# Cross-attention of a decoder layer: weighted sums in four groups of three chunks per batch, and a fourth buffer for the exponentials

## The chip, the cores and the metric

The kernel runs on one NeuronCore of one Trainium2 chip. The metric is the device time of one execution in microseconds (us); the median of three runs is compared. The engines are named as the profile names them: PE is TensorE's matmul stream and PEld its weight loads, DVE is VectorE, ACT is ScalarE, POOL is GpSimd, SP is SyncE, which here issues the DMAs.

## What is computed

One post-norm decoder layer on 32 batches of 56 tokens of 128 features: a self-attention, a cross-attention over 1500 context rows of 96 features, and a mixture of eight experts, each followed by a residual and a layer norm. The change lies in the cross-attention alone:

```python
q = (query @ Wq + bq).reshape(B, Nq, 16, 8).transpose(0, 2, 1, 3)
k = (key_value @ Wk + bk).reshape(B, Nkv, 16, 8).transpose(0, 2, 1, 3)
v = (key_value @ Wv + bv).reshape(B, Nkv, 16, 8).transpose(0, 2, 1, 3)
attn = jnp.clip(jnp.einsum('bhqd,bhkd->bhqk', q, k) * 8 ** -0.5, -CLAMP, CLAMP)
attn = jax.nn.softmax(attn, axis=-1)
x = jnp.einsum('bhqk,bhkd->bqhd', attn, v).reshape(B, Nq, 128)
return x @ Wo + bo
```

## The kernel before

The kernel has one instruction stream per engine, written out by hand, with a semaphore wait wherever one engine needs another. The cross-attention is a software pipeline of *periods*, one for each batch b (two more at the front and one behind). Each engine's function `period(b, par, half)` walks through twelve *slots*, c = 0 to 11, one for each *chunk* of 125 context rows. In slot c of period b, PE does the following in this order:

- **Scores** (L1063): four matmuls of 125 x 224 give the scores of chunk c into one of two pairs of PSUM banks. They wait until the exponential of chunk c-2 is done (semaphore `weights_ready`), since that frees the pair of banks.
- **Pieces** (L1049): the row maximum that softmax subtracts is found a batch ahead. It takes 21 *pieces* per batch, each one matmul of 128 x 500 into bank 0 or 1 and one reduction by DVE (L752, `taken`). The tables `EARLY_PIECES`, `MID_PIECES` and `LATE_PIECES` say which piece is done in which slot, and where in it: early is right after the scores, mid is after the projections, late is at the slot's end. There are only two banks, so piece n waits until the reduction of piece n-2 is done (`piece_max_taken`). Piece 1 uses bank 0 like piece 0 and waits for the reduction of piece 0. Piece 2 waits for `max_row_ready`.
- **Value projection** (L1088, slots 3, 9, 11) and **key projection** (L1097, slots 5, 6, 8) for a later batch. All of them write bank 7, as does the spread of the softmax sums (L1076, slot 0), which DVE inverts with two reciprocals (L775) in slots 0 and 1. The value projection of slot 3 waits until both reciprocals are done (`sums_inverted`).
- **The turn** (L1101, slot 8): a small matmul that transposes the row maxima, with 7 columns of weights. It waits for the last reduction of the row maxima (L763).
- **Weighted sums** (L1113 and L1117), chunk by chunk as the table `OUTPUTS` says: for chunk k four matmuls of 168 columns and four of 56, whose weights are 25 and 9 columns wide and which write the partitions from 0, 32, 64 and 96 of bank 6. They wait for the exponential of chunk k.

ACT in slot c takes the exponential of chunk c (L563) into the buffer `P2[c % NP]`, for which it waits until the weighted sum of chunk c - NP has been made; it also copies keys (L576, L578; slots 4, 6, 7) and values (L592, L593; slots 3, 9, 11) out of PSUM. The dependences around the change are these lines:

```python
if not (isinstance(b, int) and b == 0 and c < NP):
    act.wait_ge(F["outputs_made"], b * NC + (c + 1 - NP) + PRIME)
...
pe.wait_ge(F["weights_ready"], b * NC + (k + 1) + PRIME)
weights_, values = P2[k % NP], V2[par]
```

DVE in slot c reduces the early and mid pieces of that slot, then does what else the slot has (the row maximum in slot 7, the negated maxima L768 in slot 8, a reciprocal in slots 0 and 1, the scaling L778 in slot 5), and then the late pieces. POOL forms the low parts of the keys (L462) and spreads the queries (L474, L481); SP moves keys, contexts and maxima by DMA a batch ahead.

Of the kernel before, what the change touches and what calls it, by code (L numbers as in the profile page):

```python
# [51 lines left out]
EARLY_PIECES = {0: (9,), 1: (10,), 2: (11,), 3: (12,), 4: (14,), 6: (18,), 7: (20,), 9: (2,), 10: (4,), 11: (6,)}  # L52
MID_PIECES = {3: (13,), 5: (15, 16), 6: (19,), 8: (0,), 9: (3,), 11: (7,)}
LATE_PIECES = {5: (17,), 8: (1,), 10: (5,), 11: (8,)}
OUTPUTS = {2: (0, 1), 5: (2, 3, 4), 8: (5, 6, 7), 10: (8,), 11: (9, 10, 11)}
NP = 3
SLOTS = 4
FC = FF // 128
NEG = -3.0e38
# [16 lines left out]
def decoder_kernel(nc, gate_rows, x, ctx_in, wq, wk, wv, xWq, xbq, xWk, xbk, xWv, xbv, xWo, xbo, Wr, W1, W2, out):  # L76
# [8 lines left out]
    with stack:  # L85
# [44 lines left out]
        def at(parts, *shape, place=None):  # L130
            n = math.prod(shape)
            o = used[0]
            used[0] += n
            place = whole if place is None else place
            assert used[0] <= place.shape[-1], used[0]
            v = place[0:parts, o:o + n]
            if len(shape) == 2:
                v = v.rearrange("p (a b) -> p a b", b=shape[1])
            elif len(shape) == 3:
                v = v.rearrange("p (a b c) -> p a b c", b=shape[1], c=shape[2])  # L140
            return v
# [40 lines left out]
        used[0] = start  # L182
        P2 = [at(CK, HQ) for _ in range(NP)]
        O_sb = at(128, SLOTS * S)
# [133 lines left out]
        def has(b, ahead):  # L318

            return not isinstance(b, int) or 0 <= b + ahead < B  # L320
# [204 lines left out]
        def _(act):  # L525
# [26 lines left out]
            def period(b, par, half):  # L552
                for c in range(NC):
# [5 lines left out]
                    if has(b, 0):  # L559
                        act.wait_ge(F["scores_made"], b * NC + (c + 1) + PRIME)  # L560
                        if not (isinstance(b, int) and b == 0 and c < NP):
                            act.wait_ge(F["outputs_made"], b * NC + (c + 1 - NP) + PRIME)
                        a.activation(P2[c % NP].rearrange("p (n k) -> p n k", n=2), psum[0:CK, 2 + 2 * (c % 2):4 + 2 * (c % 2), 0:HQ // 2], ACT.Exp)\  # L563
                         .then_inc(F["weights_ready"], 1)
# [396 lines left out]
        def _(pe):  # L961
# [90 lines left out]
            def period(b, par, half):  # L1052
                for c in range(NC):
# [48 lines left out]
                    if has(b, 0):  # L1102
                        for k in OUTPUTS.get(c, ()):
                            if k == 0:
# [5 lines left out]
                            pe.wait_ge(F["weights_ready"], b * NC + (k + 1) + PRIME)  # L1110
                            weights_, values = P2[k % NP], V2[par]
                            for m in range(4):
# [202 lines left out]
```

## Time and profile before

| | us |
|---|---|
| median of 3 runs (1046.09 to 1053.0) | 1047.92 |
| the profiled execution, its own time | 1049.38 |
| its span in the trace | 1047.6 |
| PE busy in the span | 964.7 |
| DVE busy | 727.3 |
| ACT busy | 636.2 |
| POOL busy | 354.5 |

The periods of the cross-attention take the span from about 63 to 798 us. The self-attention and the projections stand before them, the output projection and the experts behind. The starts and durations in the timeline are those of the trace; a matmul's start is the time at which its stream begins or is queued behind the one before it, so the distance from one start to the next says more than its duration.

### The profile page before, as it was taken

To read this page: it belongs to the slowest core of one execution; us is meant where nothing else is said; L and a number is where in the kernel's file an instruction comes from. 1 tells how busy PE (TensorE), PEld (TensorE's weight loads), DVE (VectorE), ACT (ScalarE), POOL (GpSimd) and SP (SyncE) were. 2 spreads that over 40 slices of the span, in tenths; PEclk is the share of its full clock that TensorE was granted. 3 is DMA by queue.
4 is the path that set the end of the run, shared out by engine and by line. 5 is a ranking of instruction groups with operands and counts; after the bars stand their busy time and mean duration, and the time that the engine had idled before them with its cause. 6 is when DMAs were issued, how large, how long until landed. Compare 5 with 4: busy or idle time off the path is not lost.

```text
span 1047.6 us, 29217 instructions
## 1 busy us (share of the span) xinstructions
PE 964.7 (92%) x10560; PEld 776.5 (74%) x10560; DVE 727.3 (69%) x1428; ACT 636.2 (61%) x1030; POOL 354.5 (34%) x325
## 2 busy tenths in 40 slices
PE   6579999999999999999999999999995678999993
PEld 5445778778778887787787788877874367989993
DVE  2775777777777777777777677777751457777996
ACT  3303777777777777777777777777763123445551
POOL 7315333322333322333223333223300151117842
PEclk9855999999999999999999999999997859999997
DMA  3058655566655666555666556665441010105201
GB/s 97 0 113 177 133 129 112 121 143 144 143 110 110 137 145 140 128 110 118 150 140 143 110 110 139 143 142 128 90 90 43 0 41 8 34 3 199 88 35 35
DMA packets 41572, 109.55 MB, mean 105 GB/s; under 512 B 15218, under 2 KB 23732, under 8 KB 41524
## 3 DMA queue, kind: packets, MB, share of 16 engines
q1 hardware_dynamic: 41524, 108.93, 46.3%
q8 instruction: 28, 0.46, 0.2%
q14 instruction: 20, 0.16, 0.1%
HBM read 31.32 MB, written 0.97 MB: 31 GB/s over the span
## 4 chain that ended last, share of the span: by engine, by line
PE 79%; DVE 7%; issue 5%; POOL 4%; SPq 2%; DMA 2%; ACT 1%; POOLq 0%; DVEq 0%; ACTq 0%
PE psum L1063 17%; PE psum L1049 17%; PE psum L1113 12%; PE psum L1088 8%; PE psum L1097 8%; PE psum L1117 4%; POOL OS_all L518 3%; PE psum L1179 2%; PE psum L1222 2%; PE psum L1223 1%; PE psum L1224 1%; PE psum L1076 1%; DMA arena<-gate_rows 1%; PE psum L1234 1%; PE psum L1233 1%
## 5 line engine op out<-in xcount | busy, mean ns | idle before, releaser
L752 DVE TENSOR_REDUCE arena<-psum 128x1 f32<-128x500 f32 x672 | 445.6, 672 | 198.9 <-PE psum L1049 198.8
L563 ACT ACTIVATE arena<-psum 125x896 f32<-125x896 f32 x384 | 348.0, 916 | 98.9 <-PE psum L1063 90.9
L1049 PE MATMUL psum<-K_hi,Q_bd 128*128 128x500 f32 x672 | 323.1, 492 | 6.1 <-DVE arena L752 3.5
L462 POOL TENSOR_TENSOR arena<-arena,K_hi 128x500 fp32r<-128x500 f32 x96 | 123.8, 1291 | 399.4 <-ACT K_hi L578 397.5
L1063 PEld LDWEIGHTS psum<-Q_st,K_st 97*125 97x125 f32 x1536 | 221.8, 189 | 30.9 <-issue 10.9
L1063 PE MATMUL psum<-Q_st,K_st 97*125 97x224 f32 x1536 | 241.6, 280 | 2.8 <-ACT arena L563 1.3
L1049 PEld LDWEIGHTS psum<-K_hi,Q_bd 128*128 128x128 f32 x672 | 130.9, 196 | 56.8 <-issue 28.4
L1113 PE MATMUL psum<-arena 125*25 125x168 f32 x3072 | 169.4, 310 | 0.2
L637 ACT ACTIVATE K_st<-psum 128x448 fp32r<-128x448 f32 x128 | 69.7, 545 | 87.2 <-PE psum L1224 86.7
L1117 PE MATMUL psum<-arena 125*9 125x56 f32 x3072 | 117.1, 213 | 0.0
L1088 PEld LDWEIGHTS psum<-WvA,arena 97*125 97x125 f32 x768 | 103.5, 195 | 4.2
L1117 PEld LDWEIGHTS psum<-arena 125*9 125x9 f32 x3072 | 94.2, 91 | 15.6
L1088 PE MATMUL psum<-WvA,arena 97*125 97x128 f32 x768 | 103.9, 280 | 0.0
L1097 PE MATMUL psum<-arena,WkA 97*128 97x500 f32 x186 | 96.6, 601 | 0.8 <-ACT arena L576 0.8
L1113 PEld LDWEIGHTS psum<-arena 125*25 125x25 f32 x3072 | 69.1, 103 | 33.7 <-issue 32.2
L857 DVE SCALAR_TENSOR_TENSOR K_st<-psum,K_st 128x448 fp32r<-128x448 f32 x128 | 75.1, 617 | 15.2 <-ACT K_st L637 14.9
L481 POOL TENSOR_TENSOR Q_st<-arena,four_heads 96x896 fp32r<-96x896 f32 x32 | 53.7, 1678 | 78.3 <-PE psum L1063 57.5
L576 ACT COPY arena<-psum 128x500 f32<-128x500 f32 x93 | 53.8, 578 | 41.2 <-PE psum L1049 21.7
L592 ACT COPY arena<-psum 125x384 f32<-125x384 f32 x96 | 46.7, 487 | 39.6 <-PE psum L1088 36.3
L775 DVE RECIPROCAL arena<-psum 128x112 f32<-128x112 f32 x64 | 53.8, 842 | 19.6 <-PE psum L1076 19.6
L578 ACT CAST K_hi<-arena 128x500 fp32r<-128x500 f32 x93 | 56.7, 609 | 3.0
L1222 PE MATMUL psum<-K_hi,K_st 128*128 128x448 f32 x128 | 51.2, 400 | 6.1 <-issue 4.1
(246 smaller groups left out, 1056.5 us busy)
## 6 DMA issues: line engine op xcount, KB each, us to landing
K_st<-K_hi SPq DMA_DIRECT2D x256, 187.5 KB, 4.7
K_st<-arena SPq DMA_DIRECT2D x128, 187.5 KB, 3.4
arena<-in_ctx SPq DMA_DIRECT2D x32, 562.5 KB, 6.8
arena<-gate_rows SPq DMA_DIRECT2D x8, 896.0 KB, 4.3
arena<-in_L_ffn_W SPq DMA_DIRECT2D x16, 256.0 KB, 3.1
Q_st<-max_row SPq DMA_DIRECT2D x224, 0.5 KB, 1.7
arena<-K_st SPq DMA_DIRECT2D x12, 224.0 KB, 4.8
out<-x_all SPq DMA_DIRECT2D x4, 224.0 KB, 2.5
```

The source lines that it names most:

```text
L462: g.tensor_tensor(low.bitcast(F32R), low, K_hi[:, par, n * KB:n * KB + KB].bitcast(F32), ALU.subtract).then_inc(F["keys_low"], 1)
L563: a.activation(P2[c % NP].rearrange("p (n k) -> p n k", n=2), psum[0:CK, 2 + 2 * (c % 2):4 + 2 * (c % 2), 0:HQ // 2], ACT.Exp)\
L637: a.activation(h_hi[k % 2][:, f], bank[f][:, 0:QC], ACT.Relu).then_inc(S4["hidden_high"], 1)
L752: v.reduce_max(mx[:, n // NB, n % NB:n % NB + 1], bank_of(n)[:, 0:KB], AX.X).then_inc(F["piece_max_taken"], 1)
L857: v.scalar_tensor_tensor(h_lo[k % 2][:, f], bank[f][:, 0:QC], 0.0, h_hi[k % 2][:, f].bitcast(F32), ALU.max, ALU.subtract)\
L1049: mm(bank_of(n)[:, 0:KB], Q_bd[:, p].rearrange("p h q -> p (h q)")[:, 128 * (n // NB):128 * (n // NB) + 128], K_hi[:, p, (n % NB) * KB:(n ...
L1063: last = mm(bank[2 + 2 * (c % 2) + g // 2][0:CK, 4 * S * (g % 2):4 * S * (g % 2) + 4 * S], K_st[0:DC + 1, par, g, c * CK:c * CK + CK], Q_s ...
L1088: last = mm(bank[7][0:CK, 128 * k:128 * k + 128], ctxT2[:, (par + ahead) % 2, CK * q:CK * q + CK], WvA[:], start=True, stop=True)
L1097: mm(bank[7][:, 0:KB], WkA[:], ctxT2[:, par, n * KB:n * KB + KB], start=True, stop=True).then_inc(F["keys_made"], 1)
L1113: mm(bank[6][32 * m:32 * m + V3, 0:3 * S], values[:, k, V3 * m:V3 * m + V3], weights_[:, 3 * S * m:3 * S * m + 3 * S], start=(k == 0), sto ...
L1117: last = mm(bank[6][32 * m:32 * m + V1, 3 * S:4 * S], values[:, k, 4 * V3 + V1 * m:4 * V3 + V1 * m + V1], weights_[:, (12 + m) * S:(13 + m ...
L1222: mm(bank[f][:, 0:QC], w1_hi[p[0]][:, w_cols], x_hi[:, cols], start=True, stop=False)
```

## The change

Two constants change. `OUTPUTS`, which had five groups of weighted sums of 2, 3, 3, 1 and 3 chunks (slots 2, 5, 8, 10, 11), has four of three chunks (slots 3, 6, 9, 11). `NP`, the number of buffers for the exponentials, goes from 3 to 4; the buffer stands in SBUF, in the arena that the phases share.

```diff
-OUTPUTS = {2: (0, 1), 5: (2, 3, 4), 8: (5, 6, 7), 10: (8,), 11: (9, 10, 11)}
-NP = 3
+OUTPUTS = {3: (0, 1, 2), 6: (3, 4, 5), 9: (6, 7, 8), 11: (9, 10, 11)}
+NP = 4
```

Every instruction stays; on PE the weighted sums stand elsewhere. On DVE, POOL and SP the order is the same, and on ACT one wait becomes one for a smaller number. Three places on PE follow. A row is a group of instructions of one form; a chunk's weighted sum is one row of L1113 and one of L1117.

PE, slots 2 and 3 of a period, before: scores of chunk 2, piece 11, two chunks, then slot 3 with its scores, piece 12, the value projection and piece 13, and the scores of slot 4.

```order
L1063 MATMUL psum<-Q_st,K_st 125x224 x4
L1049 MATMUL psum<-K_hi,Q_bd 128x500
L1113 MATMUL psum<-arena 25x168 x4
L1117 MATMUL psum<-arena 9x56 x4
L1113 MATMUL psum<-arena 25x168 x4
L1117 MATMUL psum<-arena 9x56 x4
L1063 MATMUL psum<-Q_st,K_st 125x224 x4
L1049 MATMUL psum<-K_hi,Q_bd 128x500
L1088 MATMUL psum<-WvA,arena 125x128 x4
L1049 MATMUL psum<-K_hi,Q_bd 128x500
L1063 MATMUL psum<-Q_st,K_st 125x224 x4
```

The same place now, up to the first of the three chunks that stand at the end of slot 3:

```order
L1063 MATMUL psum<-Q_st,K_st 125x224 x4
L1049 MATMUL psum<-K_hi,Q_bd 128x500
L1063 MATMUL psum<-Q_st,K_st 125x224 x4
L1049 MATMUL psum<-K_hi,Q_bd 128x500
L1088 MATMUL psum<-WvA,arena 125x128 x4
L1049 MATMUL psum<-K_hi,Q_bd 128x500
L1113 MATMUL psum<-arena 25x168 x4
L1117 MATMUL psum<-arena 9x56 x4
```

The two chunks that stood between piece 11 and the scores of slot 3 are gone from there.

PE, slot 5 from its scores on, before: key projection, pieces 15 and 16, three chunks, piece 17, and the scores of slot 6.

```order
L1063 MATMUL psum<-Q_st,K_st 125x224 x4
L1097 MATMUL psum<-arena,WkA 128x500
L1049 MATMUL psum<-K_hi,Q_bd 128x500 x2
L1113 MATMUL psum<-arena 25x168 x4
L1117 MATMUL psum<-arena 9x56 x4
L1113 MATMUL psum<-arena 25x168 x4
L1117 MATMUL psum<-arena 9x56 x4
L1113 MATMUL psum<-arena 25x168 x4
L1117 MATMUL psum<-arena 9x56 x4
L1049 MATMUL psum<-K_hi,Q_bd 128x500
L1063 MATMUL psum<-Q_st,K_st 125x224 x4
```

The same place now, on through slot 6 to its first chunk (pieces 18 and 19 around the key projection):

```order
L1063 MATMUL psum<-Q_st,K_st 125x224 x4
L1097 MATMUL psum<-arena,WkA 128x500
L1049 MATMUL psum<-K_hi,Q_bd 128x500 x3
L1063 MATMUL psum<-Q_st,K_st 125x224 x4
L1049 MATMUL psum<-K_hi,Q_bd 128x500
L1097 MATMUL psum<-arena,WkA 128x500
L1049 MATMUL psum<-K_hi,Q_bd 128x500
L1113 MATMUL psum<-arena 25x168 x4
L1117 MATMUL psum<-arena 9x56 x4
```

Pieces 15, 16 and 17 now stand side by side, and the three chunks come after piece 19.

PE, slot 8, before: key projection, piece 0, the turn, three chunks, piece 1, and the scores of slot 9.

```order
L1097 MATMUL psum<-arena,WkA 128x500
L1049 MATMUL psum<-K_hi,Q_bd 128x500
L1101 MATMUL psum<-ident,arena 7x128
L1113 MATMUL psum<-arena 25x168 x4
L1117 MATMUL psum<-arena 9x56 x4
L1113 MATMUL psum<-arena 25x168 x4
L1117 MATMUL psum<-arena 9x56 x4
L1113 MATMUL psum<-arena 25x168 x4
L1117 MATMUL psum<-arena 9x56 x4
L1049 MATMUL psum<-K_hi,Q_bd 128x500
L1063 MATMUL psum<-Q_st,K_st 125x224 x4
```

The same place now, on to piece 2, the value projection of slot 9 and piece 3:

```order
L1097 MATMUL psum<-arena,WkA 128x500
L1049 MATMUL psum<-K_hi,Q_bd 128x500
L1101 MATMUL psum<-ident,arena 7x128
L1049 MATMUL psum<-K_hi,Q_bd 128x500
L1063 MATMUL psum<-Q_st,K_st 125x224 x4
L1049 MATMUL psum<-K_hi,Q_bd 128x500
L1088 MATMUL psum<-WvA,arena 125x128 x4
L1049 MATMUL psum<-K_hi,Q_bd 128x500
```

Only the turn stands between piece 0 and piece 1. In slot 10, pieces 4 and 5, which had one chunk between them, stand side by side as well.

## Rows read from the trace of the kernel before

**Rows 1.** The page: busy time by engine, granted clock in 40 slices, chain by engine.
```profile
PE 964.7 (92%) x10560; PEld 776.5 (74%) x10560; DVE 727.3 (69%) x1428; ACT 636.2 (61%) x1030; POOL 354.5 (34%) x325
...
PEclk9855999999999999999999999999997859999997
...
PE 79%; DVE 7%; issue 5%; POOL 4%; SPq 2%; DMA 2%; ACT 1%; POOLq 0%; DVEq 0%; ACTq 0%
```

**Rows 2.** Windows: us, PE, PEld, DVE, ACT, POOL busy (xcount), PEclk, DMA share, GB/s.
```profile
340.00:540.00 200.00, 200.00 (x2662) 159.56 (x2661) 144.53 (x245) 149.36 (x235) 64.99 (x46) 1.00 0.60 130
...
797.00:850.00 53.00, 28.93 (x116) 18.91 (x105) 20.38 (x78) 7.06 (x14) 11.81 (x11) 0.70 0.07 21
```

**Rows 3.** Timeline of PE: start, us, what; slots 0 to 5 of one period.
```profile
432.43 0.54 PE L1076 MATMUL psum<-arena,sum_rows 128*128 128x224 f32 x2
...
433.99 0.40 PE L1049 MATMUL psum<-K_hi,Q_bd 128*128 128x500 f32 x1
434.31 0.49 PE L1113 MATMUL psum<-arena 125*25 125x168 f32 x8
...
434.71 0.47 PE L1113 MATMUL psum<-arena 125*25 125x168 f32 x8
...
435.21 0.69 PE L1063 MATMUL psum<-Q_st,K_st 97*125 97x224 f32 x4
435.74 0.40 PE L1049 MATMUL psum<-K_hi,Q_bd 128*128 128x500 f32 x1
435.98 1.04 PE L1088 MATMUL psum<-WvA,arena 97*125 97x128 f32 x8
...
439.57 0.49 PE L1113 MATMUL psum<-arena 125*25 125x168 f32 x8
...
440.85 0.50 PE L1049 MATMUL psum<-K_hi,Q_bd 128*128 128x500 f32 x1
```

**Rows 4.** Timeline of PE, slots 8 to 11 of that period and the next L1076.
```profile
444.49 0.78 PE L1049 MATMUL psum<-K_hi,Q_bd 128*128 128x500 f32 x1
445.19 0.28 PE L1101 MATMUL psum<-ident,arena 128*7 128x128 f32 x1
...
446.66 0.50 PE L1049 MATMUL psum<-K_hi,Q_bd 128*128 128x500 f32 x1
...
449.19 0.39 PE L1049 MATMUL psum<-K_hi,Q_bd 128*128 128x500 f32 x1
449.52 0.49 PE L1113 MATMUL psum<-arena 125*25 125x168 f32 x8
...
450.03 0.49 PE L1049 MATMUL psum<-K_hi,Q_bd 128*128 128x500 f32 x1
450.37 0.60 PE L1063 MATMUL psum<-Q_st,K_st 97*125 97x224 f32 x4
450.80 0.39 PE L1049 MATMUL psum<-K_hi,Q_bd 128*128 128x500 f32 x1
...
454.68 0.54 PE L1076 MATMUL psum<-arena,sum_rows 128*128 128x224 f32 x2
```

**Rows 5.** Timeline of DVE in the same period, with idle time before a row.
```profile
434.52 0.84 DVE L775 RECIPROCAL arena<-psum 128x112 f32<-128x112 f32 x1
...
439.45 1.26 DVE L752 TENSOR_REDUCE arena<-psum 128x1 f32<-128x500 f32 x2 [0.83 <-PE psum L1049]
...
445.39 0.68 DVE L752 TENSOR_REDUCE arena<-psum 128x1 f32<-128x500 f32 x1 [0.70 <-PE psum L1049]
...
448.96 1.34 DVE L752 TENSOR_REDUCE arena<-psum 128x1 f32<-128x500 f32 x2 [0.42 <-PE psum L1049]
```

**Rows 6.** Timelines of ACT and of the weight loads, slots 0 to 2.
```profile
432.48 2.78 ACT L563 ACTIVATE arena<-psum 125x896 f32<-125x896 f32 x3 [0.49 <-PE psum L1063]
...
433.45 0.51 PEld L1063 LDWEIGHTS psum<-Q_st,K_st 97*125 97x125 f32 x4
```

**Rows 7.** Every instruction of L752 and the weight loads of L1049 in the page.
```profile
L752 DVE TENSOR_REDUCE arena<-psum x672: 615/679/681, 64.5 to 775.2; 128x1 f32<-128x500 f32 x168
...
L1049 PEld LDWEIGHTS psum<-K_hi,Q_bd 128*128 128x128 f32 x672 | 130.9, 196 | 56.8 <-issue 28.4
```

## The prediction

> **What bounds the kernel now.** I read the page first, then the windows, then the timelines of one period. The page shows that PE is busy for 92% of the span and holds 79% of the chain of waits [rows 1]. In the window of 200 us from the middle of the cross-attention PE is busy for 200.00 us at the full clock of 2.4 GHz, granted 1.00, while DVE is busy for 144.53 and ACT for 149.36 [rows 2]. So in this stage PE alone sets the time, and what counts is how far each PE instruction starts after the one before. A period takes 454.68 - 432.43 = 22.25 us [rows 3, 4], and there are 32 of them with weighted sums. DVE has 28% of its time free, but it is called in bursts: a reduction takes 0.68 us [rows 7], and a piece of PE only about 0.24 (435.74 to 435.98 [rows 3]). Two pieces may be under way (two banks), so a third one right behind them has to wait for DVE. In the kernel before, the weighted sums stand just where such a wait would be and fill it.
>
> **Part 1: what the weighted sums cost PE.** A lone chunk takes 450.03 - 449.52 = 0.51 us; two take 0.40 + 0.50, three 440.85 - 439.57 = 1.28 [rows 3, 4]. Going into a group, the piece ahead of it takes 0.33 us instead of 0.24 (449.19 to 449.52), and the operation behind it takes 0.10 longer than elsewhere: scores 0.53 instead of 0.43 (435.21 to 435.74, against 450.37 to 450.80), a piece 0.34 instead of 0.24 [rows 3, 4]. So one chunk within a group is 0.385, and a group costs about 0.32 on top: 0.09 in front, 0.13 inside, 0.10 behind.
> Taken out: slot 2 0.09 + 0.90 + 0.10 = 1.09; slot 5 0.09 + 1.28 + 0.10 = 1.47; slot 10 0.09 + 0.51 + 0.10 = 0.70. In slot 8 the turn, whose weights are 7 columns wide, runs with the chunks as one group [rows 4]. It stays there, and I take it that it keeps the cost of going in and out, so only 3 x 0.385 = 1.15 leave. The sum is 4.41 us. Put in: three groups of three at 1.47 = 4.41. The program has one group of chunks fewer, but the turn is now a group by itself: five before, five after. The work of PE comes out at nothing saved; at the other end the turn alone costs no passage, and 0.32 per period is gained.
> The Trainium skill, "TensorEngine Tiling (Array Packing)", Key Properties, states that a change of the array's tiling mode drains TensorE. That rule agrees with the extra 0.32 per group, and counted over the groups of the table alone it would speak for this change: a mode change fewer per period. It is the first rival below.
>
> **Part 2: the waits that lose their cover.** For each I take the time at which the releaser ends in the trace, add 0.05 for the semaphore, and compare it with when PE would arrive. The 0.05 is from slot 2: the first exponential ends at 432.48 + 0.92 = 433.40, the weights for the scores that wait for it are loaded from 433.45 [rows 6]. An operation that waits also shows its weight load: a piece behind a group, whose load could not go ahead, lasts 0.50 instead of 0.40 [rows 3], so 0.10 more. The bounds of each are without both additions below, and with the whole load of 0.19 shown above (130.9 us over 672 loads [rows 7]).
> - *Slot 5, piece 17.* Piece 15 is reduced from 439.45 to 439.45 + 0.68 = 440.13 [rows 5, 7]. Piece 17 started at 440.85; without 1.28 and 0.09 ahead of it and with its load hidden it would start at 439.48. It starts at 440.18 + 0.10: 0.80 us lost (0.65 to 0.89).
> - *Slot 8, piece 1.* It waits for piece 0, reduced from 445.39 to 446.07 [rows 5]. It started at 446.66 and would come at 446.66 - 1.15 = 445.51. It starts at 446.12: 0.61 lost (0.56 to 0.70). Its load was shown before as well, so nothing is added.
> - *Slot 3, value projection.* It waits for the second reciprocal, over at 434.52 + 0.84 = 435.36 [rows 5]. It started at 435.98 and would come at 434.89. It starts at 435.41 + 0.10: 0.62 lost (0.47 to 0.71). The scores of slot 3 wait on the way for the exponential of chunk 1, which ends near 432.48 + 2 x 0.93 = 434.34 [rows 6]; what they lose, this wait would have taken anyway.
> - *Slot 11, piece 6.* It waits for piece 4, the second of the pair of reductions that ends at 448.96 + 1.34 = 450.30 [rows 5]. It started at 450.80 and would come at 450.10. It starts at 450.35 + 0.10: 0.35 lost (0.20 to 0.44).
> Together 2.38 us per period (1.88 to 2.74). A wait further up cannot shorten one further down here: each releaser is an operation that PE itself started shortly before, in slot 3 through L1076 of slot 0, so a shift moves both. What stands behind the waiting piece on PE is the next chunk's scores, and for these ACT waits; ACT has a quarter of its time free, so it follows.
>
> **Part 3: the fourth buffer.** With NP = 3 the exponential of chunk 5 waited for the weighted sum of chunk 2, and so on. The new groups come up to one slot later, and the fourth buffer loosens this by one chunk: exponential 4 needs sum 0, which stands in slot 3, exponential 7 needs sum 3 in slot 6, exponential 10 needs sum 6 in slot 9. All of these stand ahead of the scores that the exponential needs as well. I count nothing, and the other end is also nothing: ACT's wait in the rows is for the scores [rows 6]. Without the fourth buffer nothing would be shorter either. The chunks of slot 6 need exponential 5, which ACT starts after two key copies; the scores of slot 6, pieces 18 and 19 and a key projection, more than 1.5 us, stand ahead of them. DMAs keep their places; the keys are moved a batch ahead.
>
> **The sum.** Periods 1 to 29 have all four waits: 29 x 2.38 = 69.0. Period 0 has no sums of an earlier batch, so no reciprocals: 1.76. Period 30 has only pieces 9 to 20: 0.80 + 0.62 = 1.42. Period 31 has none, but keeps about 0.3 of the scores' wait in slot 3. The total is 72.5 us. Against the profiled execution, 1049.38 + 72.5 = 1121.9. The median of the runs is 1.46 below that execution: 1047.92 + 72.5 = 1120.4. The bounds by period give 30 x 1.88 = 56 and 30 x 2.74 = 82, so 1104 to 1130. The forecast is **1120.4 us**, 6.9% slower.
>
> **The rivals.**
> - *A group fewer, and nothing waits (faster).* Place: the passages in and out of the groups. If the turn alone costs no passage and the pieces find DVE ready, each of 31 periods gains 0.32: 1047.9 - 10 = 1038. For it: DVE is 28% idle, and before the pieces hardly waited. Against it: piece 17 would come at 439.48, but the reduction it needs ends at 440.13 whatever PE does. It decides only if each of the four waits is under 0.08. 3%.
> - *Only the two back-to-back waits count (slots 5 and 8).* If the waits of slots 3 and 11, whose margins are smaller, vanish: 30 x 1.41 = 42, so 1090. For it: those two have the widest relative bounds. Against it: the second reciprocal ends 0.5 us after PE would arrive. 8%.
> - *The waits compound.* Each shows its whole load of 0.19, and bunched pieces push DVE later in slots 6 and 7, where piece 18 comes 0.7 us behind 17 and the reduction itself takes 0.68. At 0.5 us more per period: 1120.4 + 15 = 1135. 12%.
> - *The clock falls.* Gaps of up to 0.8 us open in a stage that had none. In a window with PE busy for 28.93 of 53 us the granted clock was 0.70 [rows 2]. Here PE would stay busy for nine tenths, so I expect 1.00; if a tenth of the stage's 700 us ran at 1.2 GHz, it would do half the work there, 35 us: 1155. 3%.
> - *The forecast itself*: 71%. A time within 1% of before (a mixture of partly hidden waits): 3%.
>
> **Range and chances.** The bounds 1104 to 1130 hold the forecast's own range; I widen to 1100 and 1136 to take in the compounding rival and part of the one with two waits. About 1% is what a measurement of this kernel can tell from no change. Faster by over 1% is 3%, within 1% is 3%, slower by over 1% is 94%.
>
> **What would show it.** In the changed profile DVE and ACT keep their busy time, and PE waits for DVE L752 ahead of L1049 some 90 times, for about 50 us in total, mostly on its weight loads. The period is near 24.5 us. Pieces 15 and 17 start 1.5 us apart, pieces 0 and 1 1.6 us, and L1088 of slot 3 starts right when the second L775 ends. L1101 alone still shows its 0.32. The time outside the stage and the clock in it do not change. A period under 23.5 us, or a piece 17 that follows 16 after 0.24 us, would prove the forecast wrong.

## The result, and the profile after

The changed kernel takes 1122.99 us (median of four runs, 1122.78 to 1124.06), the kernel before beside it 1047.22 us (1046.09 to 1053.0). The ratio is 1.071, with a 95% interval of 1.068 to 1.073. The forecast was 1120.4 us, with a range of 1100 to 1136. The profiled execution of the changed kernel has a span of 1121.3 us, against 1047.6.

The page of the changed kernel: busy times, the granted TensorE clock in 40 slices, the shares of the chain of waits, and the weight loads of the pieces (busy, mean ns of one | idle time ahead of them and what ended it).

```profile
PE 996.5 (89%) x10560; PEld 767.7 (68%) x10560; DVE 716.9 (64%) x1428; ACT 631.0 (56%) x1030; POOL 354.7 (32%) x325
...
PEclk9658999999999999999999999999999768999997
...
PE 70%; DVE 13%; issue 6%; POOL 3%; ACT 3%; SPq 2%; DMA 2%; DVEq 0%; POOLq 0%; ACTq 0%
...
L1049 PEld LDWEIGHTS psum<-K_hi,Q_bd 128*128 128x128 f32 x672 | 128.0, 195 | 115.3 <-DVE arena L752 80.0
```

The work of DVE, ACT and POOL is nearly what it was (DVE 716.9 after 727.3, ACT 631.0 after 636.2, [rows 1]). PE's share of the span falls from 92 to 89%, and in the chain PE goes from 79 to 70% while DVE goes from 7 to 13%. The last line says where: PE's weight loads for the pieces idle for 80.0 us behind the reductions of L752. PE's busy time itself rises from 964.7 to 996.5 us with the same 10560 matmuls. The record of a piece lasts 0.40 us, though the next matmul can start 0.24 behind its start, so the first part of each wait counts as busy. The clock in the stage stays at its full level, but for some 3 us in its last period.

The windows of the changed kernel: the same 200 us in the middle of the stage as [rows 2], and 100 us behind the stage's last pieces. The columns are busy time (count) of PE, PEld, DVE, ACT and POOL, then granted clock, DMA share and GB/s.

```profile
340.00:540.00 200.00, 189.49 (x2421) 142.15 (x2420) 127.11 (x219) 132.75 (x212) 58.02 (x41) 1.00 0.55 119
...
850.00:950.00 100.00, 66.81 (x524) 51.25 (x512) 39.98 (x131) 28.97 (x47) 19.14 (x17) 0.76 0.08 22
```

PE was busy for all 200 us and now idles for 10.5 of them at a granted 1.00. That understates the loss, for the reason just given: 2421 matmuls get done instead of 2662, 9% fewer. DVE and ACT drop with it, since less is done in the same time. So no other engine became the bound by its load. The stage is held by waits.

The waits of the changed kernel: who waited on which tile and line for whom; us in total, times, longest.

```profile
PEld psum L1049 <- DVE arena L752: 80.0, 131, 1.3
...
PE psum L1049 <- DVE arena L752: 38.2, 71, 1.9
...
PEld psum L1063 <- ACT arena L563: 15.3, 35, 0.8
...
PEld psum L1088 <- DVE arena L775: 9.4, 30, 0.4
```

The first of these in the kernel before:

```profile
PEld psum L1049 <- DVE arena L752: 15.8, 43, 1.1
```

The other three stood below 4 us there or did not appear. So 88 waits of a piece's weight load are new, for 64 us, and 30 of the value projection for the second reciprocal. One more wait is new: the weight loads of L1113 idle for 15.4 us (35 times, 0.6 us before) for the exponentials of L563, mostly in slot 6. It costs PE nothing: in e2 below it is 1.2 us in 4 waits, and the periods are as long.

Four timelines follow, all of one period in the middle of the stage: start, duration, engine, line, count, and in brackets the idle time and what ended it. First PE, slots 2 and 3, slot 5, slot 8 and slots 10 and 11, then the start of the next period:

```profile
465.53 0.54 PE L1076 MATMUL psum<-arena,sum_rows 128*128 128x224 f32 x2
...
467.08 0.40 PE L1049 MATMUL psum<-K_hi,Q_bd 128*128 128x500 f32 x1
467.60 0.70 PE L1063 MATMUL psum<-Q_st,K_st 97*125 97x224 f32 x4
468.13 0.40 PE L1049 MATMUL psum<-K_hi,Q_bd 128*128 128x500 f32 x1
468.52 1.14 PE L1088 MATMUL psum<-WvA,arena 97*125 97x128 f32 x8
...
472.75 1.01 PE L1049 MATMUL psum<-K_hi,Q_bd 128*128 128x500 f32 x2
474.31 0.49 PE L1049 MATMUL psum<-K_hi,Q_bd 128*128 128x500 f32 x1 [0.55 <-DVE arena L752]
...
479.41 0.78 PE L1049 MATMUL psum<-K_hi,Q_bd 128*128 128x500 f32 x1
480.11 0.39 PE L1101 MATMUL psum<-ident,arena 128*7 128x128 f32 x2
481.04 0.50 PE L1049 MATMUL psum<-K_hi,Q_bd 128*128 128x500 f32 x1 [0.54 <-DVE arena L752]
...
485.05 0.63 PE L1049 MATMUL psum<-K_hi,Q_bd 128*128 128x500 f32 x2
485.52 0.60 PE L1063 MATMUL psum<-Q_st,K_st 97*125 97x224 f32 x4
486.22 0.50 PE L1049 MATMUL psum<-K_hi,Q_bd 128*128 128x500 f32 x1
...
490.21 0.54 PE L1076 MATMUL psum<-arena,sum_rows 128*128 128x224 f32 x2
```

DVE, the reductions and reciprocals that release these:

```profile
467.63 0.84 DVE L775 RECIPROCAL arena<-psum 128x112 f32<-128x112 f32 x1
...
473.58 1.26 DVE L752 TENSOR_REDUCE arena<-psum 128x1 f32<-128x500 f32 x2 [0.84 <-PE psum L1049]
...
480.31 0.68 DVE L752 TENSOR_REDUCE arena<-psum 128x1 f32<-128x500 f32 x1 [0.70 <-PE psum L1049]
...
485.49 1.95 DVE L752 TENSOR_REDUCE arena<-psum 128x1 f32<-128x500 f32 x3 [1.47 <-PE psum L1049]
```

And the weight loads that wait:

```profile
467.60 0.51 PEld L1063 LDWEIGHTS psum<-Q_st,K_st 97*125 97x125 f32 x4 [0.42 <-ACT arena L563]
...
468.52 0.95 PEld L1088 LDWEIGHTS psum<-WvA,arena 97*125 97x125 f32 x8 [0.30 <-DVE arena L775]
...
474.31 0.19 PEld L1049 LDWEIGHTS psum<-K_hi,Q_bd 128*128 128x128 f32 x1 [0.97 <-DVE arena L752]
...
481.04 0.19 PEld L1049 LDWEIGHTS psum<-K_hi,Q_bd 128*128 128x128 f32 x1 [0.83 <-DVE arena L752]
...
486.22 0.19 PEld L1049 LDWEIGHTS psum<-K_hi,Q_bd 128*128 128x128 f32 x1 [0.29 <-DVE arena L752]
```

Read them against [rows 3] and [rows 4]. Piece 17 (474.31) is loaded 0.73 us after the reduction of piece 15 began at 473.58, that is, one reduction of 0.68 and the 0.05 of a semaphore. Piece 1 (481.04) stands just so behind the reduction of piece 0 (480.31 + 0.68 = 480.99). The value projection of slot 3 (468.52) starts 0.05 behind the second reciprocal (467.63 + 0.84 = 468.47). Piece 6 (486.22) is the fourth: the first of the three reductions from 485.49, that of piece 4, is over at 486.17. The period is 490.21 - 465.53 = 24.68 us; periods alternate between 24.50 and 24.68, as they alternated between 22.07 and 22.25 before.

**Where the 73.7 us of span come from.** The first scores start at 95.9 us instead of 98.3: 2.4 earlier, in the front, where the clock changes level. Period 0, from the first scores to the first L1076, takes 120.7 - 95.9 = 24.8 us instead of 122.1 - 98.3 = 23.8. From the first L1076 to the last it is 872.0 - 120.7 = 751.3 instead of 798.1 - 122.1 = 676.0: 75.3 more. Behind it 249.3 instead of 249.5. Together -2.4 + 1.0 + 75.3 - 0.2 = 73.7. The 75.3 are 31 intervals: 29 whole periods 2.41 longer (69.9), three of these, which the code writes out instead of looping over, another 0.73 each (2.2), period 30 by 1.4 (19.92 for 18.54) and period 31 by 1.8 (16.22 for 14.38).

### The profile page after: what moved, and what is told of

Its sections match the earlier page's. It is cut to its first block, busy times and chain, and to the rows that moved or that the text cites. A ratio compares the mean times of both kernels' runs of the same rounds, so it can differ in the third digit from the quotient of the medians.

```text
span 1121.3 us, 29216 instructions
## 1 busy us (share of the span) xinstructions
PE 996.5 (89%) x10560; PEld 767.7 (68%) x10560; DVE 716.9 (64%) x1428; ACT 631.0 (56%) x1030; POOL 354.7 (32%) x325
## 4 chain that ended last, share of the span: by engine, by line
PE 70%; DVE 13%; issue 6%; POOL 3%; ACT 3%; SPq 2%; DMA 2%; DVEq 0%; POOLq 0%; ACTq 0%
PE psum L1063 14%; PE psum L1049 13%; PE psum L1113 11%; PE psum L1088 8%; PE psum L1097 7%; DVE arena L752 7%; PE psum L1117 3%; ACT arena L563 3%; POOL OS_all L518 2%; PE psum L1222 2%; PE psum L1179 1%; PE psum L1223 1%; PE psum L1224 1%; PE psum L1233 1%; PE psum L1234 1%
## 5 line engine op out<-in xcount | busy, mean ns | idle before, releaser
L752 DVE TENSOR_REDUCE arena<-psum 128x1 f32<-128x500 f32 x672 | 438.8, 671 | 281.4 <-PE psum L1049 281.2
L563 ACT ACTIVATE arena<-psum 125x896 f32<-125x896 f32 x384 | 342.3, 915 | 151.2 <-PE psum L1063 147.2
L1049 PE MATMUL psum<-K_hi,Q_bd 128*128 128x500 f32 x672 | 316.3, 489 | 44.2 <-DVE arena L752 38.2
L1063 PE MATMUL psum<-Q_st,K_st 97*125 97x224 f32 x1536 | 250.2, 286 | 6.0 <-ACT arena L563 1.3
L1063 PEld LDWEIGHTS psum<-Q_st,K_st 97*125 97x125 f32 x1536 | 213.4, 188 | 39.9 <-ACT arena L563 15.3
L1049 PEld LDWEIGHTS psum<-K_hi,Q_bd 128*128 128x128 f32 x672 | 128.0, 195 | 115.3 <-DVE arena L752 80.0
L1113 PE MATMUL psum<-arena 125*25 125x168 f32 x3072 | 162.0, 311 | 0.6 <-ACT arena L563 0.4
L1117 PE MATMUL psum<-arena 125*9 125x56 f32 x3072 | 108.8, 213 | 0.0
L1088 PEld LDWEIGHTS psum<-WvA,arena 97*125 97x125 f32 x768 | 100.2, 193 | 12.3 <-DVE arena L775 9.4
L1088 PE MATMUL psum<-WvA,arena 97*125 97x128 f32 x768 | 106.2, 283 | 0.3
L1117 PEld LDWEIGHTS psum<-arena 125*9 125x9 f32 x3072 | 86.3, 92 | 18.9
L1113 PEld LDWEIGHTS psum<-arena 125*25 125x25 f32 x3072 | 63.5, 104 | 37.7 <-issue 21.8
L775 DVE RECIPROCAL arena<-psum 128x112 f32<-128x112 f32 x64 | 53.8, 844 | 21.1 <-PE psum L1076 21.1
```

The source lines that it names most:

```text
L752: v.reduce_max(mx[:, n // NB, n % NB:n % NB + 1], bank_of(n)[:, 0:KB], AX.X).then_inc(F["piece_max_taken"], 1)
L1049: mm(bank_of(n)[:, 0:KB], Q_bd[:, p].rearrange("p h q -> p (h q)")[:, 128 * (n // NB):128 * (n // NB) + 128], K_hi[:, p, (n % NB) * KB:(n ...
L1063: last = mm(bank[2 + 2 * (c % 2) + g // 2][0:CK, 4 * S * (g % 2):4 * S * (g % 2) + 4 * S], K_st[0:DC + 1, par, g, c * CK:c * CK + CK], Q_s ...
L1088: last = mm(bank[7][0:CK, 128 * k:128 * k + 128], ctxT2[:, (par + ahead) % 2, CK * q:CK * q + CK], WvA[:], start=True, stop=True)
L1113: mm(bank[6][32 * m:32 * m + V3, 0:3 * S], values[:, k, V3 * m:V3 * m + V3], weights_[:, 3 * S * m:3 * S * m + 3 * S], start=(k == 0), sto ...
L1117: last = mm(bank[6][32 * m:32 * m + V1, 3 * S:4 * S], values[:, k, 4 * V3 + V1 * m:4 * V3 + V1 * m + V1], weights_[:, (12 + m) * S:(13 + m ...
```

## The experiments

The theory under test: the time goes into four waits (for DVE three times at L752 and once at L775), each with its own price, because the weighted sums no longer stand in front of the waiting instruction. The rivals on record: passages in and out of the groups (the time that PE loses when it goes from other matmuls to a group of weighted sums and back), the buffer, a price that compounds. Later a further question came up, the 0.73 us of the written-out periods. All ratios are to the kernel before on the same chip. Each "period" is the shorter of the two between which the distance of L1076 alternates in the loop: 22.07 before, 24.50 after.

| run | edit, on | us | ratio (95%) | period |
|---|---|---|---|---|
| e1 | buffer alone, before | 1047.11 | 0.998 (0.996 to 1.000) | 22.07 |
| e2 | groups alone, after | 1123.98 | 1.072 (1.069 to 1.076) | 24.49 |
| e3 | slot 5's sums to 6, before | 1073.48 | 1.023 (1.018 to 1.027) | 22.88 |
| e4 | slot 8's sums to 9, before | 1076.08 | 1.028 (1.024 to 1.032) | 23.00 |
| e5 | slot 2's sums to 3, before | 1071.81 | 1.020 (1.016 to 1.024) | 22.71 |
| e6 | reduction over half the columns, after | 1089.11 | 1.037 (1.033 to 1.041) | 23.46 |
| e7 | four groups that keep the cover, before | 1038.40 | 0.990 (0.986 to 0.993) | 21.75 |
| e8 | turn behind the group, before | 1067.24 | 1.015 (1.011 to 1.020) | 22.56 |
| e9 | e7 with three buffers | 1054.82 | 1.007 (1.004 to 1.010) | 22.28 |
| e10 | scaling in slot 4, after | 1115.03 | 1.065 (1.062 to 1.067) | 24.49 |
| e11 | the changed kernel again | 1122.98 | 1.071 (1.068 to 1.075) | 24.51 |
| e12 | e7 with scaling in slot 4 | 1040.21 | 0.992 (0.990 to 0.995) | 21.76 |

**The two halves of the change.** e1 takes the buffer alone, e2 the groups alone.

```diff
 # e1, on the kernel before
-NP = 3
+NP = 4
 # e2, on the changed kernel
-NP = 4
+NP = 3
```

> The groups of before with four buffers. If the time comes from pieces and the value projection that lost their cover (theory W), the buffer does nothing: within 0.3% of before, 1047 us, period 22.1 to 22.25 us. If the fourth buffer itself costs something on ACT or in the arena (rival B), part or all of the 76 us shows here.

> The new groups with three buffers. Theory W: the same waits as in the changed kernel, 1123 us, period 24.5 to 24.7, since each exponential's releasing sum stands ahead of it either way. If the fourth buffer is needed for the new groups (rival N), the exponentials of chunks 3 to 5 wait for the sums at the end of slot 3 and PE waits for them: over 1128 us.

e1 moves the time by 0.2%, no more than a measurement can tell, and e2 is as slow as the whole change. The loss lies in the places of the weighted sums alone.

**One group at a time.** e3, e4 and e5 move one group of the kernel before, all with four buffers.

```diff
 # e3
-OUTPUTS = {2: (0, 1), 5: (2, 3, 4), 8: (5, 6, 7), 10: (8,), 11: (9, 10, 11)}
+OUTPUTS = {2: (0, 1), 6: (2, 3, 4), 8: (5, 6, 7), 10: (8,), 11: (9, 10, 11)}
 # e4 (the line that goes is the same)
+OUTPUTS = {2: (0, 1), 5: (2, 3, 4), 9: (5, 6, 7), 10: (8,), 11: (9, 10, 11)}
 # e5 (the same)
+OUTPUTS = {3: (0, 1), 5: (2, 3, 4), 8: (5, 6, 7), 10: (8,), 11: (9, 10, 11)}
```

> Of the change only one move: the sums of chunks 2, 3, 4 from slot 5 to slot 6 (four buffers). Theory W: piece 17 loses its cover and waits for the reduction of piece 15, 0.80 us in 31 periods, 25 us: 1072 us. The number of groups stays five, so a theory that counts passages in and out of groups (rival P) expects no change, 1047.

> Only one move: the sums of chunks 5, 6, 7 from slot 8 to slot 9, so that the turn stands alone and piece 1 comes right behind it. Theory W: piece 1 waits for the reduction of piece 0 (0.61 us), and there is one passage more, six groups with the turn, of about 0.32 us, of which the wait may hide 0.1: 0.82 to 0.93 us in 30 periods, 1072 to 1075 us. If the turn alone costs no passage: 0.61, 1065 us. If only passages count and no wait: 1057 us.

> Only one move: the sums of chunks 0 and 1 from slot 2 to slot 3 (four buffers). Theory W: scores and value projection of slot 3 wait for the exponential of chunk 1 and for the second reciprocal, 0.62 to 0.78 us in 31 periods: 1066 to 1071 us. Rival P (passages only, still five groups): 1047.

The waits of e3, then those of e4 and of e5 (same columns as above):

```profile
PEld psum L1049 <- DVE arena L752: 49.5, 75, 1.3
```

```profile
PEld psum L1049 <- DVE arena L752: 37.9, 70, 1.1
```

```profile
PEld psum L1049 <- DVE arena L752: 16.2, 44, 1.1
...
PEld psum L1063 <- ACT arena L563: 14.5, 35, 0.7
...
PEld psum L1088 <- DVE arena L775: 9.4, 30, 0.4
```

Of the four waits each run shows those of its own slot and no others: 32 more of L1049 than the 43 before in e3, 27 more in e4, one more in e5, which has those of L1063 and L1088 in their place. The periods grow by 0.81, 0.92 and 0.64. The 0.92 of e4 is a wait of 0.61 and a passage of 0.31, since moving the three chunks leaves the turn alone and makes a group more. The split is read from e4's rows: piece 1 starts 0.92 behind the turn, and what stands behind a turn that nothing holds up starts 0.31 behind it (e8 below, 454.86 to 455.17). The three runs add up to 2.37. What is left of the change is that the single chunk of slot 10 joins a group: it saves 0.32 and puts piece 6 into a wait of 0.37. 2.37 + 0.05 = 2.42, and the period of the changed kernel is 2.43 longer. So the waits neither overlap nor compound. (The 0.37 is read from the changed kernel itself; no run has this wait alone.)

**Is it the length of the reduction?** e6 reduces the first 250 of a piece's 500 columns; the other half of each row maximum is left out.

```diff
-v.reduce_max(mx[:, n // NB, n % NB:n % NB + 1], bank_of(n)[:, 0:KB], AX.X).then_inc(F["piece_max_taken"], 1)
+v.reduce_max(mx[:, n // NB, n % NB:n % NB + 1], bank_of(n)[:, 0:KB // 2], AX.X).then_inc(F["piece_max_taken"], 1)
```

> The changed kernel with reductions that read 250 of a piece's 500 columns (left out: half of the scores that the row maximum is taken over). A reduction should take about 0.42 us instead of 0.68. Theory W: the waits of pieces 17, 1 and 6 shrink by 0.26 each and the second reciprocal ends earlier, so the period falls by 1.0 to 1.3 us: 1123 - 30 to 38, or 1085 to 1093 us. If PE itself is slower in the new order (rival P), the time stays at 1123.

The waits of e6:

```profile
PEld psum L1049 <- DVE arena L752: 52.8, 118, 0.8
```

A reduction falls from 0.68 to 0.42 us, the loads' waits from 80.0 to 52.8, and the period by 1.04, to 23.46. In the middle of the stage DVE is now busy for 88.62 of 200 us, and PE still waits for it. It is when a reduction starts and how long that one takes that counts, not DVE's load.

**Fewer groups with the cover kept.** The rival that a group fewer gains 0.32 per period could not show in the change, where the turn takes the place of the fifth group. e7 leaves slots 2, 5 and 8 alone and joins the chunk of slot 10 to those of slot 11, with the pieces of slots 10 and 11 set so that nothing waits.

```diff
-EARLY_PIECES = {0: (9,), 1: (10,), 2: (11,), 3: (12,), 4: (14,), 6: (18,), 7: (20,), 9: (2,), 10: (4,), 11: (6,)}
-MID_PIECES = {3: (13,), 5: (15, 16), 6: (19,), 8: (0,), 9: (3,), 11: (7,)}
-LATE_PIECES = {5: (17,), 8: (1,), 10: (5,), 11: (8,)}
-OUTPUTS = {2: (0, 1), 5: (2, 3, 4), 8: (5, 6, 7), 10: (8,), 11: (9, 10, 11)}
-NP = 3
+EARLY_PIECES = {0: (9,), 1: (10,), 2: (11,), 3: (12,), 4: (14,), 6: (18,), 7: (20,), 9: (2,), 10: (4,), 11: (5,)}
+MID_PIECES = {3: (13,), 5: (15, 16), 6: (19,), 8: (0,), 9: (3,), 11: (6, 7)}
+LATE_PIECES = {5: (17,), 8: (1,), 11: (8,)}
+OUTPUTS = {2: (0, 1), 5: (2, 3, 4), 8: (5, 6, 7), 11: (8, 9, 10, 11)}
+NP = 4
```

> Four buffers and groups of 2, 3, 3, 4 chunks in slots 2, 5, 8, 11: one group fewer than before, with the cover of slots 2, 5 and 8 kept, the turn inside a group, and pieces 5 and 6 moved to slot 11 around its value projection. Theory W with 0.32 us per passage in and out: faster than before by 31 x 0.32 = 10 us, 1037 us, period 21.75 to 21.93. If a passage costs nothing, 1047.

The same window of e7:

```profile
340.00:540.00 200.00, 200.00 (x2678) 161.21 (x2676) 144.98 (x246) 150.37 (x238) 64.83 (x45) 1.00 0.62 133
```

PE is busy for all 200 us again and gets 2678 matmuls done in them, 16 more than before [rows 2]. The period is 0.32 shorter, and the kernel takes 1038.40 us, faster than both. It is 1% below the kernel before (0.990, 0.986 to 0.993). The edit moves two pieces besides, so it alone does not single out the passage. But e4 and e8 give the passage the same price, and "four groups" was not the mistake. e9 takes its fourth buffer away:

```diff
 # e9, on e7
-NP = 4
+NP = 3
```

> The kernel of e7 with three buffers. Chunk 8's sum is now in the same group as chunk 11's, and with three buffers the exponential of chunk 11 waits for it: the sum of chunk 11 waits about 0.26 us for the exponential, so of the 10 us some 8 are lost: 1045 us. If a fourth buffer is of no use anywhere: 1037 us as e7.

ACT and PE in slot 11 of e9, the third and the fourth chunk of the group:

```profile
458.14 0.92 ACT L563 ACTIVATE arena<-psum 125x896 f32<-125x896 f32 x1 [1.92 <-PE psum L1117]
...
458.22 0.47 PE L1113 MATMUL psum<-arena 125*25 125x168 f32 x8
...
459.12 0.49 PE L1113 MATMUL psum<-arena 125*25 125x168 f32 x8 [0.33 <-ACT arena L563]
```

The exponential of chunk 11 starts only when the first sum of the group (L1117) has freed its buffer, and PE's fourth chunk waits for it: 0.90 from the one before instead of 0.38. The size was missed, 0.26 expected and 0.51 seen, since PE comes to it in the middle of a group and the exponential itself lasts 0.92. The period is 0.53 longer than in e7, and the time as a whole is above that of the kernel before (1.007, 1.004 to 1.010). A buffer that does nothing in one order (e1, e2) is worth 31 x 0.53 = 16 us in another.

**The turn alone.** e8 moves the turn of the kernel before behind the group and piece 1, so that it is a group by itself, while the chunks keep their place.

```diff
 # e8, in slot 8 of the kernel before: these lines go
 # from ahead of the weighted sums to behind the late pieces
 if c == TURN_SLOT and has(b, 1):
     pe.wait_ge(F["row_max_taken"], b + 2 + PRIME)
     mm(bank[1][0:RG, 0:128], m2x, ident[:], start=True, stop=True).then_inc(F["max_transposed"], 1)
```

> The kernel before with the turn moved behind piece 1, out of the group of sums, nothing else. If the turn alone pays its own passage in and out of a group: +0.32 us in 31 periods, 1057 us. If it costs a passage only with the sums: 1047.

The end of slot 8 and the start of slot 9 in e8 (L1120 is the turn there); PE, then DVE and the load that waits:

```profile
454.86 0.39 PE L1120 MATMUL psum<-ident,arena 128*7 128x128 f32 x2
...
455.17 0.70 PE L1063 MATMUL psum<-Q_st,K_st 97*125 97x224 f32 x4
...
455.38 0.28 DVE L768 TENSOR_SCALAR max_row<-psum 7x128 fp32r<-7x128 f32 x1 [1.35 <-PE psum L1120]
...
455.77 0.19 PEld L1049 LDWEIGHTS psum<-K_hi,Q_bd 128*128 128x128 f32 x1
455.80 0.47 PE L1049 MATMUL psum<-K_hi,Q_bd 128*128 128x500 f32 x1
```

The period grows by 0.48 instead of the 0.32 expected, and the time by 16 us (1.015) instead of 10. 0.31 of it is the lone turn. The other 0.17 is piece 2 at 455.80, which waits for the negated maxima (L768, over at 455.66); with the turn late they are late too. Piece 2 starts 0.63 behind the scores, where 0.53 is the distance behind a group, and the value projection 0.31 behind piece 2 instead of 0.24. The passage is confirmed, and the edit brought a wait of its own that the expectation had overlooked.

**The written-out periods.** Three periods of the changed kernel last 25.23 us instead of 24.50. Here is slot 6 of one of them, starting with the scaling (L778) that DVE does for slot 5:

```profile
794.20 1.26 POOL L462 TENSOR_TENSOR arena<-arena,K_hi 128x500 fp32r<-128x500 f32 x1 [11.28 <-ACT K_hi L578]
794.30 1.39 DVE L778 SCALAR_TENSOR_TENSOR OS_all<-arena 128x224 f32<-128x224 f32 x1
...
795.63 1.93 DVE L752 TENSOR_REDUCE arena<-psum 128x1 f32<-128x500 f32 x3
...
796.35 0.49 PE L1049 MATMUL psum<-K_hi,Q_bd 128*128 128x500 f32 x1 [0.49 <-DVE arena L752]
```

and the same place of a period in the loop:

```profile
745.29 0.38 DVE L778 SCALAR_TENSOR_TENSOR OS_all<-arena 128x224 f32 x1
745.43 1.34 POOL L462 TENSOR_TENSOR arena<-arena,K_hi 128x500 fp32r<-128x500 f32 x1 [11.58 <-ACT K_hi L578]
```

The scaling takes 0.38 us where it starts ahead of POOL's subtraction, and 1.39 where it starts 0.10 behind it: it ends at 795.69, some 0.2 after the subtraction at 795.46. This is so in every copy of the code: in the three long ones the subtraction leads by 0.10 to 0.12, and in all 26 periods of the loop the scaling leads, by 0.11 to 0.14, and the subtraction then takes 1.34 to 1.38 instead of 1.25. The reductions behind it are late, and piece 19 waits for them. The Trainium skill, "SBUF — State Buffer", Who interferes with whom, says that a DVE instruction with two SBUF inputs contends with a GpSimd instruction that reads SBUF and that the order of issue decides who blocks; the trace agrees as to which of the two is slowed in both places. e10 puts the scaling one slot earlier in the changed kernel, away from the subtraction.

```diff
-                    if c == 5 and has(b, -1):
+                    if c == 4 and has(b, -1):
```

> The changed kernel with DVE's scaling (L778) moved from slot 5 to slot 4. In the changed kernel three periods, those written out at the ends of the loop, last 25.2 us instead of 24.6; in them L778 takes 1.39 us instead of 0.38 beside a subtraction of POOL that began just before it. If the two share a path: L778 takes 0.38 in all periods and these three fall to 24.6, 2 us in all, 1121 us. If the long L778 has another cause, it stays.

> The changed kernel once more, beside the kernel before and e12. It tells whether the 8 us by which e10 was below it (2 us of them expected) are the program's or the day's. If the rest of 6 us comes from the clock granted behind the cross-attention, which e10's profile shows at half speed for 31 us and the changed kernel's for 48, and if that goes by where the stage ends: 1123 us again, 48 us at half speed again.

> e7 with DVE's scaling in slot 4. In e7, as in the kernel before, no piece waits for DVE, so the long L778 of the written-out periods is hidden: its periods stay at 21.76 us and the time at 1038 us. If the scaling costs something there too: up to 2 us less.

All durations of L778 (min/median/max ns) in the changed kernel:

```profile
L778 DVE SCALAR_TENSOR_TENSOR OS_all<-arena x32: 380/382/1391, 129.9 to 874.0; 128x224 f32 x26, 128x224 f32<-128x224 f32 x6
```

and in e10:

```profile
L778 DVE SCALAR_TENSOR_TENSOR OS_all<-arena x32: 379/381/392, 127.5 to 869.7; 128x224 f32 x26, 128x224 f32<-128x224 f32 x6
```

The long ones are gone in e10, and the three periods fall to 24.49: 3 x 0.73 = 2.2 us, as expected. But e10 took 1115.03 us where some 1121 were expected. The rest does not lie in the whole periods. The last 100 us of the table above, in the changed kernel, had a granted clock of 0.76; here they are in e10:

```profile
850.00:950.00 100.00, 66.00 (x503) 52.10 (x495) 47.72 (x158) 32.02 (x53) 21.54 (x20) 0.85 0.08 22
```

and in e11, the changed kernel once more, whose profiled execution took 1117.93 us:

```profile
850.00:950.00 100.00, 66.97 (x568) 52.53 (x567) 44.88 (x150) 33.52 (x54) 19.17 (x17) 0.85 0.08 22
```

A granted 0.76 means 48 of these 100 us at the lower level of 1.2 GHz, 0.85 means 30. e11 has the same program as the changed kernel, and its periods are the same (24.51, and the long ones 25.22 to 25.24). Its expectation was 48 us at the lower clock again, and the profiled execution had 30. Behind the last L1076 it is 6.0 us shorter, and in period 31 it is 1.5 shorter (14.69 us for 16.22): there the clock of the first profile had already fallen for some 3 us (granted 0.92 from 850 to 872 us, in e11 1.00). In the front it lost 2.3, which leaves the 5 us. So that difference comes with the execution and not with an edit. All four runs of e10 are low, however (1113.04 to 1116.95), and of the eight of the changed kernel only one is, the one profiled in e11; whether the edit makes the short stretch likelier stays open. e12 puts the scaling in slot 4 of e7, where its wait was covered anyway: the period stays at 21.76, and 1040.21 us is not distinguishable from e7. e7 stays the best version measured.

## Why the prediction was right

- **Part 1** (taken out 4.41, put in 4.41, the turn keeps its passage) held. The turn alone at slot 8 costs 0.31 (e4, e8), and with it inside a group and one group fewer the gain of 0.32 appears (e7). The Trainium skill, "TensorEngine Tiling (Array Packing)", Key Properties, says that a change of the tiling mode drains TensorE; it gives no price. The runs agree that going in and out costs something, though none shows that it is the drain, and nothing was saved here: the number of groups did not fall.
- **Part 2, slot 5**: predicted 0.80. From piece 16 to 17 it is now 0.933 instead of 0.235, and the scores follow piece 17 after 0.332 instead of 0.235 (medians of 29 periods and more): 0.80. e3 alone gives 0.81.
- **Slot 8**: predicted 0.61. From the turn to piece 1 it is 0.93, where a turn without a wait takes 0.31 (e8): 0.62. e4 gives 0.92 less 0.31, so 0.61.
- **Slot 3**: predicted 0.62. From piece 11 to the scores, within the scores, and on to and through the value projection 0.64 is added; e5 gives 0.64. As the prediction had it, the scores wait for ACT on the way (0.28), and that is part of the 0.64 and not on top.
- **Slot 11**: predicted 0.35, measured 0.37: from the scores to piece 6 it is 0.70 instead of 0.43, and on to the value projection 0.33 instead of 0.23. It was not tried by itself.
- **Part 3** (the buffer counts nothing) held, by e1 and e2.
- **The sum** by period was 2.38 and is 2.41 to 2.43. Three terms were missed or too small. In the spans (73.7 longer, where 72.5 were forecast) they are in part offset by chance: the profiled execution of the kernel before took 2.4 us longer up to the first scores, and 1.1 in period 0. With the missed terms, which follow, it adds up: 72.5 + 2.2 + 1.5 + 0.4, and 0.9 for 29 periods at 2.41 instead of 2.38, less 3.5 for these two and 0.2 behind the stage, is 73.8. The written-out periods lose 0.73 each, 2.2 us in all: the prediction took DVE's other work to be where it was and missed that L778 lasted 1.39 us in a few periods of the kernel before as well. There the weighted sums ahead of piece 17 covered it. Period 31 lost 1.8 instead of 0.3; in e11 it lost 0.3 (14.69 us), so the rest belongs to an execution whose clock fell a little earlier. In period 0 the predicted 1.76 is not visible as such: 1.0 is seen, but the kernel before took 1.1 us longer there for its first three slots, at the lower clock (from the first scores to piece 11 it takes 101.52 - 98.29 = 3.23, after the change 98.01 - 95.87 = 2.14). Beside e1, which started that period at the full clock as the changed kernel did, it is 24.80 - 22.68 = 2.1. The 0.37 above the forecast is the scores' wait of slot 3, which is there without the reciprocals too (e5 shows it alone: 23.05 - 22.68); the forecast counted it in period 31 and not in period 0.
- **The signs named ahead.** 88 waits of weight loads were 90 in the forecast; their 64 us were 50. That is no contradiction: the idle time of a load is longer than the delay of its matmul, since the load would have gone ahead of it. The load of piece 17 idles for 0.97, and the stream loses 0.80.
- **The rivals.** Two waits only: e5 rules it out, since slot 3 costs 0.64. Compounding: the single terms add up to 2.42 of 2.43. The clock falling in the stage: it is granted 1.00 with PE busy for 189.49 of 200 us; it fell only in the last period of the changed kernel's first profile, for 1.5 us.

## What to carry to other kernels

Work that stands between two users of a small ring of buffers is cover even if it has nothing to do with them. Before it is moved, take the time at which the releaser ends, add the semaphore, and compare it with the time at which the waiting instruction would now arrive; here that gave four prices within 0.02 us each, though the engine waited for had 28% of its time free. In this kernel a grouping paid only where it left fewer changes of form in the stream, small matmuls of the same form counted in, and where every wait kept something in front of it: e7, and e12 built on it, do both and are the only versions that gain clearly. And a buffer's worth can only be told beside the order that needs it.

## What the runs showed of the hardware

- A scaling on DVE with both inputs in SBUF took 1.39 us instead of 0.38 where POOL's subtraction of 1.26 us had started 0.10 us earlier. Started ahead of it, DVE's took 0.38 and POOL's 1.34 to 1.38. 0.1 us in the order of two engines that exchange nothing is worth 1 us to one of them.
- A group of matmuls with weights of 25 and 9 columns costs PE 0.32 us in going in and out (e7, [rows 3]), and a lone transposing matmul with 7 columns of weights costs 0.31 (e4 and e8).
- The same program had 48 us at the lower clock behind the stage in one execution and 30 in another, 1123.00 us and 1117.93 us. A difference of 5 us between two profiled executions with this tail says nothing of the kernels unless that stretch is compared first.
